# Mamba layer: three of sixteen states take du*B from ScalarE and TensorE instead of VectorE

## The reference

```
u, z = split(x @ in_w.T);  u = silu(causal_conv4(u) + conv_b)
x_dbl = u @ xproj_w.T                        # 8 rows for dt, 16 for B, 16 for C
dt = softplus(x_dbl[:8] @ dt_w.T + dt_b)
dA = exp(dt * A[n]);  dBu = dt * u * B[n]    # for each state n of 16
h[t] = dA[t] * h[t-1] + dBu[t];  y[t] += h[t] * C[n][t]
y = (y + u * D) * silu(z);  out = y @ out_w.T
```

## Time and profile before

| | us |
|---|---|
| median of 3 runs (lowest to highest) | 2488.03 (2478.44 to 2491.33) |
| the profiled execution's own time | 2469.95 |
| its span, first to last instruction | 2468.2 |
| mean granted TensorE clock | 0.924 |

### The profile page before, as it was taken

One profiled execution on the slowest core, in us unless ns is written; L12 is line 12 of the kernel. 1 busy time (PEld: TensorE's weight loads), 2 busy tenths in 40 slices (PEclk: granted clock), 3 DMA queues, 4 the chain that ended last, 5 costly groups with the idle time before them and its releaser, 6 DMA issues. The chain is left out here.

```text
span 2468.2 us, 43398 instructions
## 1 busy us (share of the span) xinstructions
PE 2078.3 (84%) x13248; PEld 1323.3 (54%) x13248; DVE 1879.3 (76%) x3049; ACT 1431.6 (58%) x2678; POOL 1410.2 (57%) x1050
## 2 busy tenths in 40 slices
PE   3888888888888886899865892799999998998486
PEld 1333343334333333677643782466666666777476
DVE  5999999999999997677644334588888885777445
ACT  4667666667666662466542551466666664665254
POOL 4788788878788885333254454355545543332546
PEclk7999999999999999799986996899999998999588
DMA  4222222222222221200111222000000001000442
GB/s 122 74 76 74 74 73 74 73 73 73 73 73 72 76 75 45 74 12 12 31 39 58 82 80 79 1 1 0 0 0 0 0 1 57 12 12 13 140 143 72
DMA packets 104165, 130.67 MB, mean 53 GB/s; under 512 B 33412, under 2 KB 65462, under 8 KB 103376
## 3 DMA queue, kind: packets, MB, share of 16 engines
q1 hardware_dynamic: 95344, 111.19, 15.5%
q0 software_dynamic: 8192, 17.59, 2.0%
q10 hardware_dynamic: 512, 0.53, 0.1%
HBM read 111.16 MB, written 25.20 MB: 55 GB/s over the span
## 5 line engine op out<-in xcount | busy, mean ns | idle before, releaser
L858 POOL TENSOR_TENSOR m_hc<-m_h,m_cs 128x1024 f32<-128x1024 f32 x256 | 602.8, 2359 | 179.8 <-DVE m_h L768 165.5
L768 DVE TENSOR_TENSOR_SCAN m_h<-m_da,m_pdb 128x1024 f32<-128x1024 f32 x256 | 585.1, 2286 | 28.3 <-DVE m_pdb L740 3.9
L461 PE MATMUL m_py<-m_hc,ident 128*128 128x512 f32 x1024 | 505.2, 617 | 1.9 <-POOL m_hc L858 1.9
L643 ACT ACTIVATE m_da<-m_dt,m_aneg 128x508 f32<-128x508 f32 x512 | 331.8, 709 | 115.9 <-DVE m_h L768 103.3
L740 DVE TENSOR_TENSOR m_pdb<-m_du,m_pdb 128x1024 f32<-128x1024 f32 x256 | 309.0, 1207 | 22.8 <-PE m_pdb L448 13.7
L461 PEld LDWEIGHTS m_py<-m_hc,ident 128*128 128x128 f32 x1024 | 199.4, 197 | 220.6 <-issue 211.3
L2094 POOL TENSOR_TENSOR d_pr<-d_pr,d_rden 128x512 f32<-128x512 f32 x128 | 133.0, 1039 | 177.2 <-DVE d_rden L2025 177.2
L1111 ACT ACTIVATE x_prT<-x_pt 77x512 f32<-77x512 f32 x256 | 137.8, 586 | 132.9 <-PE x_pt L1013 132.0
L1227 POOL TENSOR_TENSOR x_kd<-x_kT,x_hm 128x308 f32<-128x308 f32 x64 | 45.1, 704 | 273.8 <-ACT x_v_raw L1123 273.8
L448 PE MATMUL m_pdb<-m_bcrow,m_sel 96*128 96x512 bf16 x256 | 100.3, 392 | 112.2 <-DVE m_h L768 112.2
L2104 POOL TENSOR_TENSOR d_r<-d_mean_sq,minus_half 128x20 f32<-128x20 f32 x32 | 113.1, 3534 | 75.8 <-DVE d_mean_sq L2051 75.8
(11 more groups left out here) (315 smaller groups left out, 4638.0 us busy)
## 6 DMA issues: line engine op xcount, KB each, us to landing
m_cs<-crow SPq DMA_DIRECT2D x256, 256.0 KB, 3.0
f_row<-f_sorted SPq DMA_DIRECT2D x24, 400.0 KB
c_row<-c_sorted SPq DMA_DIRECT2D x40, 144.0 KB
c_back_in<-c_routed SPq DMA_DIRECT2D x16, 256.0 KB, 3.3
f_sorted<-in_F_blank SPq DMA_DIRECT2D x9, 400.0 KB
cw_gud<-in_C_gud SPq DMA_DIRECT2D x1, 3456.0 KB
x<-in_x SPq DMA_DIRECT2D x8, 256.0 KB, 4.3
fw_w<-in_F_w SPq DMA_DIRECT2D x1, 2048.0 KB, 8.6
```

Of the source, the lines that this page charges most:

```text
L461: ins = mm(py[:, c, :], S.ident[:, :], hc[n % BUF][:, c, :], start=False, stop=n == NS - 1)
L643: A_(dst, src, ACT.Exp, scale=aneg[:, d, c, n:n + 1]).then_inc(s["da_ready"], 1)
L768: V.tensor_tensor_scan(h[n % BUF][:, way], da[n % BUF][:, d:d + CH * GT][:, way], pdb[:, b:b + 2, :].rearrange("p c t -> p (c t)")[:, way] ...
L858: P.tensor_tensor(hc[n % BUF][:, :, :], h[n % BUF][:, :].rearrange("p (c t) -> p c t", c=CH), bc(cs[n % BUF][:, :], 1, CH), ALU.mult).then ...
```

## The change

States 5, 7 and 10 (`TURNED`) no longer get du*B from VectorE. Instead:

- TensorE transposes du (tokens to partitions) in two parts of four 128 x 128 blocks in turns 0 and 1 into `pm[1]`, and ScalarE copies each part to `duT`.
- In turn 9, `front` turns the B rows as well: four small products with a 16 x 16 identity into `pm[1]`; ScalarE copies them to `bT`, ahead of `norm`.
- In the turned layout B[n] is one value for each partition, so ScalarE makes du*B with four activations with a scale (`weigh`), in turns 2, 3 and 5, into tiles that reuse `soft`, `relu` and `pre`.
- In place of the spread matmul, TensorE transposes the eight blocks back into the two PSUM banks from which the scan reads.
- VectorE's scan of such a state waits for TensorE; `step` does nothing.
- The skip products move from state 0 to state 10 of `add_state`, that is from turn 3 to turn 13.
- Waits are added: the next unit's first convolution product, GpSimd's du and ScalarE's Abs for buffers' reuse; the dt product for `bT`.

```diff
+    TURNED = (5, 7, 10)
+    WEIGHED_AT = {2: 5, 3: 7, 5: 10}
+    SKIP_AT = 10
+    NM, ND = len(TURNED), NS - len(TURNED)
...
+        dbT = [t[:, :, :].rearrange("p c t -> p (c t)").rearrange("p (i e) -> p i e", e=DI) for t in (soft, relu, pre)]
...
                                 pe.wait_ge(s["z_raw"], CH * u)
+                            if c == 0 and due(2 * u):
+                                pe.wait_ge(s["duT_ready"], 2 * u)
...
+                    if at in (None, 9):
+                        pe.wait_ge(s["frow_ready"], u + 1)
+                        pe.wait_ge(s["row_hi"], u + 1)
+                        for i in range(GS):
+                            ins = mm(pm[1][:, i * NS:(i + 1) * NS], frow[d][0:NS, i * T:(i + 1) * T],
+                                     S.ident[0:NS, 0:NS], start=True, stop=True)
+                        ins.then_inc(s["bT_mm"], 1)
...
                             if c == 1:
-                                pe.wait_ge(s["row_hi"], u + 1)
+                                pe.wait_ge(s["bT_ready"], u + 1)
                             mm(pm[c][:, :], W.dtw[FP_ROWS:FP_ROWS + DR, d, c * 128:(c + 1) * 128],
                                frow[d][FP_ROWS:FP_ROWS + DR, :], start=True, stop=True).then_inc(s["dt_mm"], 1)
...
+                    if n in TURNED:
+                        m = by_turn(u, n)
+                        pe.wait_ge(s["dbT_ready"], m + 1)
+                        for i in range(GS):
+                            for c in range(CH):
+                                ins = tr(pdb[:, row_bank(n) + c, i * T:(i + 1) * T],
+                                         dbT[by_turn(0, n)][:, i, c * 128:(c + 1) * 128], S.ident[:, :])
+                        ins.then_inc(s["b_mm"], 1)
+                        return
                     mm(pdb[:, row_bank(n), :], sel[:, n, :], bcrow[d][:, :],
                        start=True, stop=True).then_inc(s["b_mm"], 1)
+                def turn_du(u, d, k):
+                    if k == 0:
+                        pe.wait_ge(s["du_ready"], u + 1)
+                        pe.wait_ge(s["z_raw"], CH * (u + 1))
+                    else:
+                        pe.wait_ge(s["duT_ready"], 2 * u + 1)
+                    for i in range(2):
+                        for c in range(CH):
+                            at = (2 * k + i) * T
+                            ins = tr(pm[1][:, (2 * i + c) * 128:(2 * i + c + 1) * 128], du[d][:, c, at:at + T],
+                                     S.ident[:, :])
+                    ins.then_inc(s["duT_mm"], 1)
                 def add_state(u, n, d):
-                    if n == 0:
-                        pe.wait_ge(s["us_ready"], CH * (u + 1))
-                        if due(CH * u):
-                            pe.wait_ge(s["y1_ready"], CH * u)
-                        for c in range(CH):
-                            mm(py[:, c, :], skip[:, d, c, :], us[d][:, c, :], start=True, stop=False)
+                    if n == 0 and due(CH * u):
+                        pe.wait_ge(s["y1_ready"], CH * u)
                     for c in range(CH):
                         ins = mm(py[:, c, :], S.ident[:, :], hc[n % BUF][:, c, :],
-                                 start=False, stop=n == NS - 1)
+                                 start=n == 0, stop=n == NS - 1)
+                        if n == SKIP_AT:
+                            mm(py[:, c, :], skip[:, d, c, :], us[d][:, c, :], start=False, stop=False)
...
                             spread(u, n + 1, d)
                         elif nxt:
                             spread(u + 1, 0, 1 - d)
+                        if n < 2:
+                            turn_du(u, d, n)
                         if nxt:
                             nxt(n)
                         if n >= LAG:
...
+                    if at in (None, 9):
+                        act.wait_ge(s["bT_mm"], u + 1)
+                        A_(bT[d][:, :, :], pm[1][:, 0:GS * NS].rearrange("p (i n) -> p i n", n=NS), ACT.Copy
+                           ).then_inc(s["bT_ready"], 1)
                     if at in (None, 10):
...
                                     act.wait_ge(s["dt_ready"], u)
+                                if due(NS * (u - 1) + TURNED[-1] + 1):
+                                    act.wait_ge(s["b_mm"], NS * (u - 1) + TURNED[-1] + 1)
                             A_(pre[:, c, :], pm[c][:, :], ACT.Abs,
...
+                def keep_turned(u, k):
+                    act.wait_ge(s["duT_mm"], 2 * u + k + 1)
+                    A_(duT[:, 2 * k:2 * k + 2, :], pm[1][:, :].rearrange("p (i e) -> p i e", e=DI), ACT.Copy
+                       ).then_inc(s["duT_ready"], 1)
+                def weigh(u, n, d):
+                    k = by_turn(0, n)
+                    if k == 0:
+                        act.wait_ge(s["bT_ready"], u + 1)
+                        act.wait_ge(s["duT_ready"], 2 * (u + 1))
+                    for i in range(GS):
+                        ins = A_(dbT[k][:, i, :], duT[:, i, :], ACT.Copy, scale=bT[d][:, i, n:n + 1])
+                    ins.then_inc(s["dbT_ready"], 1)
                             decay(u + 1, 0, 1 - d)
+                        if n < 2:
+                            keep_turned(u, n)
+                        if n in WEIGHED_AT:
+                            weigh(u, WEIGHED_AT[n], d)
                         if n == 4 and not (isinstance(u, int) and u == 0):
                             sum_up(u - 1, 1 - d)
...
                 def step(u, n, d):
                     N = NS * u + n
+                    if n in TURNED:
+                        return
...
                         dve.wait_ge(s["da_ready"], CH * (N + 1))
-                        dve.wait_ge(s["db_ready"], N + 1)
+                        if n in TURNED:
+                            dve.wait_ge(s["b_mm"], N + 1)
+                        else:
+                            dve.wait_ge(s["db_ready"], by_dve(u, n) + 1)
...
                         pool.wait_ge(s["us_ready"], CH * (u + 1))
-                        if due(NS * (u - 1)):
-                            pool.wait_ge(s["db_ready"], NS * (u - 1))
+                        if due(u - 1):
+                            pool.wait_ge(s["db_ready"], by_dve(u - 1, 0))
+                            pool.wait_ge(s["duT_mm"], 2 * (u - 1))
                         P.tensor_tensor(du[d][:, :, :], dt[d][:, :, :], us[d][:, :, :],
                                         ALU.mult).then_inc(s["du_ready"], 1)
```

More of the change, by code:

```diff
@@ L297, in mamba_layer @@
         hc = [A.sb(f"hc{k}", [128, CH, GT]) for k in range(BUF)]
+        duT = A.sb("duT", [128, GS, DI])
+        bT = [A.sb(f"bT{d}", [128, GS, NS]) for d in range(2)]
         y1 = A.sb("y1", [128, CH, GT])
@@ L309, in mamba_layer @@
             du_ready skip_ready b_mm da_ready db_ready h_ready hc_ready y_mm y1_ready ys_ready o_mm
-            x_ready seg_zero aexp_ready""".split()
+            x_ready seg_zero aexp_ready bT_mm bT_ready duT_mm duT_ready dbT_ready""".split()
         s = {n: A.sem(n) for n in names}
@@ L322, in row_bank, with by_dve, by_turn @@
             return 2 * (n % 2)
+        def by_dve(u, n):
+            return ND * u + sum(m not in TURNED for m in range(n))
+        def by_turn(u, n):
+            return NM * u + sum(m in TURNED for m in range(n))
         with nc.Block() as block:
```

## The result

The change makes the kernel slower: 2521.28 us (median of 4, 2519.75 to 2527.36) against 2485.24 (4 runs), ratio 1.0157 with a 95% interval of 1.0124 to 1.019. Forecast were 2519 and +31 us; measured is +36. The profiled execution took 2521.89, its span is 2520.0; that of before took 2469.95, so the pair of traces differs by 52 us.

What follows compares the result with a forecast made beforehand. VectorE was taken to set the pace, with TensorE the later engine in turns 2 to 10. Odd units +14, even +20.3, unit 15 -3.9, first front +1 gave +31 us on 2488: 2519, range 2470 to 2550.

Steps and rivals of the forecast that it cites:

- Where the time is: VectorE sets the layer's pace, but TensorE is the later engine from turn 2 to 10; each product removed frees 1.3 us.
- TensorE's added work: Eight transposes replace a spread in turns 4, 6 and 9, +0.7 us each; turning B in turn 9 adds 0.7.
- ScalarE's turns 0 to 4: du copies and weighings queue ahead of sum_up, so TensorE's add_state of state 0 stalls 1.0 us (even units 0.4).
- The new wait: ScalarE waits in turn 9 for B's transposes, so the dt matmul comes 2.0 us later (odd units), 2.9 (even).
- The sum: Whole execution: odd units +14, even units +20.3, unit 15 -3.9, first front +1, total +31 us.
- the loss comes on top as before: Behind the dt wait the clock falls as it did already (13.7 us of VectorE's waits); no change counted.
- A: Rival, faster: turned B is ready before ScalarE needs it, its turn 9 wait ending by 32.6; -19 us, 2469; chance 0.18.
- B: Rival, no change: half of the dt matmul's shifts, with the clock no longer falling; +7 us, 2495; chance 0.15.
- C: Rival, much slower: TensorE idles in even units' dt wait, low clock reaches into next turns; +66 us, 2554; chance 0.09.

Runs made afterwards that it cites:

- x6: x1 with states 14 and 15 turned instead of 5, 7 and 10, weighings behind sum_up, skip product back in turn 3: 2381.32 us, 0.9847 of before.
- x7: x6 with GpSimd making du in turn 13 right behind dt, instead of in turn 14: 2358.26 us, 0.9759 of the kernel before.
- x1: The changed kernel with ScalarE's copy of the turned B moved from turn 9 to turn 10, behind its store of x: 2463.3 us, 0.9948 of before.
- x5: x1 with one turned state (5) instead of three (5, 7, 10): 2384.03 us, 0.9864 of the kernel before.
- x8: The kernel before the change with only the skip products moved from turn 3 to turn 13: 2419.7 us, 1.0012 of before.
- x2: The changed kernel with add_state of state 7 put ahead of the dt matmuls on TensorE in turn 10: 2490.71 us, 1.0054 of before.
- x4: The kernel before the change with add_state of state 7 put ahead of the dt matmuls in turn 10: 2465.87 us, 0.995 of before.
- x3: The changed kernel with both the edits of x1 and x2: 2485.9 us, 1.0035 of the kernel before.

## Why the prediction was right

**Where the time is.** "VectorE is given back time in turns 5, 7 and 10, where TensorE has none" holds for 7 and 10: the same removal in turns 14 and 15 pays (x6, x7), there it costs (x1 against x5). It goes too far for 5, which pays by itself (x5). And that TensorE is busy without a gap from turn 2 to 10 of the kernel before doesn't make it what holds the unit: 1.7 us less in turn 3 changed nothing (x8).

**TensorE's added work.** Transposes at 0.11 each are right, 0.87 for eight. The Trainium skill's "4× faster for FP32" ("TensorE: Matmul & The Clock Gate", Terms) is not seen in this trace, where a transpose costs half of a product. The turning of B took 0.99 where I had 0.7 and at most 0.9: passes of 16 columns cost 0.12, as much as passes of 128.

**ScalarE's turns 0 to 4.** A weighing takes 1.6 of the queue (1.7 forecast), sum_up starts at 11.2 (609.35; forecast 11.4), TensorE's stall is 0.78 (1.0). Turn 9 starts at 33.1 (631.19; 33.2 forecast).

**VectorE.** In unit 9 scan 5 at 16.2, scan 8 at 27.6, scan 10 at 34.2, scan 11 at 38.5: forecast 16.4, 27.7, 34.2 and 38.2. In units 1 to 3 and 12 to 14 scan 8 comes earlier than I said was possible, at 26.2 to 26.8 (28.0 before), and it changes nothing: scan 10 waits for its transposes all the same.

**The new wait.** Forecast dt matmul 38.4 (odd) and 39.4 (even), measured 38.5 to 38.6 and 39.5 to 39.9. x1 shows that this wait is the loss against the kernel before: with all the work kept and the wait moved, there is none. In unit 14, which has no norm behind the wait, it is 38.0; I had counted it with 2.9 and it is 1.8.

**The sum.** The shifts of the dt matmul add up to 37 us over units 1 to 14 (16 odd, 21 even), against 34 in the forecast. Unit 15 gives back 3.8, forecast 3.9. What remains of the 48.9 us in the profiled executions, about 12, is the clock, which I had put at no change and priced in the range: the wait ahead of the dt matmul is 3.0 to 3.2 us in even units 2 to 12, and there scan 12 comes at 48 to 49.5. The experiments bear out the size: filling the idle time gives back 27.0 us of the layer in the changed kernel (x2) and 12.3 in the one before (x4). So "the loss comes on top as before" is the term that was too small.

Against the medians the whole is 5 us above the forecast's +31, and that closeness is partly luck. The sum was made for the profiled execution, and on the pair of traces the layer loses 45 us, not 31; that the medians are only 36 apart comes from a profiled execution of before that was 15 us faster than its median.

**The rivals.** A needed ScalarE's wait to end by 32.6; it ended at 35.1 (633.26). B needed the clock to stay up; it fell in 13 of units 1 to 14. C had this mechanism, but priced it at 35 us where some 12 were seen.

## What to carry to other kernels

Work taken off the busiest engine pays only in the stretch where that engine sets the pace: find the turns where another engine is behind, and put the offload elsewhere. A wait added to an in-order engine costs what is queued behind it, so follow that queue to the next engine; here a copy of 0.23 us, ahead of the store of x and not behind it, cost some 50 us. Then ask what is late next: taking two products off the end of a unit gave 35 us, and 58 once du was made a turn earlier.

## What the runs showed of the hardware

TensorE's clock is not explained by the idle time just ahead. In x7 TensorE idles 0.13 us ahead of the dt matmul of unit 8 and its next 8 us run at 0.79; in unit 9 it idles not at all and the same stretch runs at 1.00, but so does that of unit 1, behind 0.27 us:

```profile
521.20:529.20 8.00, 7.98 (x15) 3.23 (x16) 6.45 (x9) 7.94 (x10) 6.29 (x4) 0.79 0.27 67
576.10:584.10 8.00, 8.00 (x20) 3.42 (x20) 7.93 (x6) 7.93 (x11) 6.45 (x4) 1.00 0.24 66
```

In x5 it falls in five of the six units that have 0.6 us of idle there, and in x2's odd units, x3 and x1, with none, not at all. In the kernel before it stays up behind 1.5 us in units 2, 9 and 11, and falls in unit 0 with no idle ahead. In x4 taking 1.5 us of idle away kept the clock up. What else decides stays open; no run here tells it apart. A pass with 16 columns costs TensorE as much of its queue as one with 128 (0.12 and 0.11).
